# Attention outputs through HBM: new layouts, fewer stores, more loads, and the row maxima stored from ScalarE's queue

## What is computed

```python
content = einsum('bhqd,bhkd->bhqk', q, k)
relative = einsum('bhqd,qkd->bhqk', q, rpk)
w = softmax((content + relative) / sqrt(hd), axis=-1)
out = einsum('bhqk,bhkd->bhqd', w, v) + einsum('bhqk,qkd->bhqd', w, rpv)
x = x + layernorm(out @ Wo.T + bo)
x = x + layernorm(shared(layernorm(x)) + expert[top1](layernorm(x)))
```

## Time and profile before

| | |
|---|---|
| median of 3 runs | 1836.75 us (1835.77 to 1839.23) |
| profiled execution, its own time | 1832.55 us |
| its span, first to last instruction | 1830.8 us |
| granted TensorE clock, mean | 0.966 |
| busy: PE, DVE, ACT, POOL | 1635.2, 1253.0, 1108.6, 539.3 us |
| DMA packets, of these under 512 bytes | 490853, 332391 |

### The profile page before, as it was taken

One profiled execution on the slowest core, in us unless ns is written; L12 is line 12 of the kernel. 1 busy time (PEld: TensorE's weight loads), 2 busy tenths in 40 slices (PEclk: granted clock), 3 DMA queues, 4 the chain that ended last, 5 costly groups with the idle time before them and its releaser, 6 DMA issues. The chain is left out here.

```text
span 1830.8 us, 64404 instructions
## 1 busy us (share of the span) xinstructions
PE 1635.2 (89%) x26621; PEld 1211.2 (66%) x26621; DVE 1253.0 (68%) x3502; ACT 1108.6 (61%) x2059; POOL 539.3 (29%) x1114
## 2 busy tenths in 40 slices
PE   2889999999999999999999999999999897867772
PEld 1337767676777777767776777767677764567762
DVE  5996667787788878777878777868662344326655
ACT  2437767676767676767676766767556652256551
POOL 5423021314132313222331323131010126523445
PEclk9999999999999999999999999999999999979886
DMA  2468855755553554445344654463345533133340
GB/s 61 141 168 204 177 162 108 200 103 158 103 145 88 120 117 114 107 110 135 85 113 102 138 101 127 91 162 49 64 91 145 141 73 103 63 112 101 97 121 29
DMA packets 490853, 211.88 MB, mean 116 GB/s; under 512 B 332391, under 2 KB 464164, under 8 KB 490560
## 3 DMA queue, kind: packets, MB, share of 16 engines
q1 hardware_dynamic: 475968, 165.77, 40.5%
q0 software_dynamic: 14592, 42.00, 6.5%
HBM read 105.73 MB, written 102.85 MB: 114 GB/s over the span
## 5 line engine op out<-in xcount | busy, mean ns | idle before, releaser
L934 ACT ACTIVATE w<-sc,escale 128x512 f32<-128x512 f32 x1024 | 687.5, 687 | 424.5 <-PE sc L731 257.4
L1135 DVE TENSOR_REDUCE mx<-mix 128x1 f32<-128x512 f32 x960 | 647.0, 685 | 265.2 <-PE mix L711 239.8
L710 PE MATMUL mix<-WE 128*128 128x512 f16 x960 | 395.4, 412 | 23.3 <-DVE mx L1135 12.8
L724 PE MATMUL sc<-QC,KC 104*128 104x128 f16 x4096 | 401.9, 221 | 7.7 <-ACT w L934 4.5
L750 PE MATMUL pv<-w,VC 128*9 128x128 f32 x8192 | 385.8, 275 | 5.4 <-issue 5.3
L724 PEld LDWEIGHTS sc<-QC,KC 104*128 104x128 f16 x4096 | 271.3, 98 | 166.6 <-issue 81.1
L711 PE MATMUL mix<-Wn,WE 128*128 128x256 f16 (+1 forms) x960 | 290.0, 302 | 0.4 <-issue 0.4
L750 PEld LDWEIGHTS pv<-w,VC 128*9 128x9 f32 x8192 | 175.9, 90 | 150.8 <-issue 133.7
L757 PE MATMUL rel<-w,Rv 128*32 128x128 f32 x5120 | 264.7, 274 | 5.1 <-issue 5.1
L731 PE MATMUL sc<-QT,Wt 96*128 96x64 f16 x5120 | 262.0, 193 | 4.8 <-issue 4.6
L925 ACT ACTIVATE WE<-qp,hmask 128x256 f16<-128x256 f16 x512 | 249.1, 500 | 24.6 <-PE sc L711 21.2
(11 more groups left out here) (224 smaller groups left out, 1834.6 us busy)
## 6 DMA issues: line engine op xcount, KB each, us to landing
qm_d<-ks POOLq DMA_DIRECT2D x48, 512.0 KB, 4.2
QT<-qm_d SPq DMA_DIRECT2D x32, 768.0 KB
kt_d<-ks SPq DMA_DIRECT2D x48, 256.0 KB
KC<-kt_d SPq DMA_DIRECT2D x128, 96.0 KB
xs_d<-zrow SPq DMA_DIRECT2D x5, 2056.0 KB, 12.3
vs_d<-vst SPq DMA_DIRECT2D x16, 576.0 KB
VC<-vs_d SPq DMA_DIRECT2D x32, 288.0 KB
orl_d<-rel_s SPq DMA_DIRECT2D x512, 8.0 KB
```

The costliest lines, as they stand in the source:

```text
L710: nc.tensor.matmul(nat[:], lq, kn[b2][:, KEYS_AT[t]:KEYS_AT[t] + S], start=True, stop=False, skip_group_check=True)
L724: mm = nc.tensor.matmul(bank[:, P * g:P * g + P], KC[j][:, b2, g, 0 if near else 1, :], qc[:, g, :, 32 * q8:32 * q8 + 32], start=(g == 0), ...
L934: nc.scalar.activation(w[tile % 2][:, slot % 4, slot // 4 % 2].rearrange("p h q -> p (h q)"), sc[slot % 2][:], ACT.Exp, scale=escale[:, 0: ...
L1135: nc.vector.tensor_reduce(mx[:, k:k + 1], nat[:], AX.X, ALU.max).then_inc(s["mx_done"], 1)
```

## The change

Plain outputs and sums go to HBM with the head's dimension first (opv_d), four stores of 9 partitions a query tile instead of eight. The relative outputs go as rel_s stands, whole partitions, in one store of 128 partitions instead of sixteen of 8. A half is loaded with 12 transfers instead of 8: four for oB that pick the wanted partitions and queries (64-byte runs), two for oA, four for oS, two for xr. oA has rows ordered by dimension and head instead of head and dimension, so the rows of Wo are put in the same order once, by an ACT copy in the set-up for which PE waits. ACT writes pv_s in pieces of 128 elements; DVE reads rel in order and writes rel_s at a stride of 64 bytes. The sum of oA and oB is two instructions. The two stores of a group of row maxima leave SP's list for ACT's, behind the exponential of the same slot (slots 1 to 113 of the turns; the first pair's groups stay on SP).

```diff
-    opv_d = dram("opv_d", [B * H, HD + 1, S], F32)
-    orl_d = dram("orl_d", [B * H * HD, S], F32)
+    opv_d = dram("opv_d", [NP, NT, HD + 1, H, 2, P], F32)
+    orl_d = dram("orl_d", [NP, NT, P, H, NU, 2, NB], F32)
-    pv_s = sb("pv_s", [P, 2, 4, P])
-    rel_s = sb("rel_s", [P, NU, 2 * H, NB])
+    pv_s = sb("pv_s", [P, 4, 2, P])
+    rel_s = sb("rel_s", [P, H, NU, 2, NB])
+    wo_rows = w_flat[0][:, S * 4 - P:S * 4]
...
         def store_o(n, t):
 
             sp.wait_ge(s["pv_ev"], 2 * (4 * n + t) + 2)
-            rows = opv_d[bass.ds(2 * n * H, 2 * H)].rearrange("(b g hh) d q -> b g d hh q", b=2, g=4)
-            for b2 in range(2):
-                for g in range(4):
-                    sp.dma_start(rows[b2, g, :, :, P * t:P * t + P], pv_s[32 * g:32 * g + HD + 1, b2]).then_inc(s["o_st"], 16)
+            for g in range(4):
+                sp.dma_start(opv_d[n, t, :, 4 * g:4 * g + 4].rearrange("d h b q -> d (h b q)"),
+                             pv_s[32 * g:32 * g + HD + 1].rearrange("d h b q -> d (h b q)")).then_inc(s["o_st"], 16)
             sp.wait_ge(s["rel_ev"], 2 * (4 * n + t) + 2)
-            dst = orl_d[bass.ds(2 * n * P, 2 * P)].rearrange("(bh d) q -> d bh q", d=HD)
-            for q32 in range(NS):
-                for u in range(NU):
-                    row = 32 * q32 + HD * (NU - 1 - u)
-                    q0 = P * t + 32 * u + NB * q32
-                    sp.dma_start(dst[:, :, q0:q0 + NB], rel_s[row:row + HD, u, :, :]).then_inc(s["o_st"], 16)
+            sp.dma_start(orl_d[n, t].rearrange("p h u b k -> p (h u b k)"), rel_s[:].rearrange("p h u b k -> p (h u b k)")).then_inc(s["o_st"], 16)
...
             q = slice(S // 2 * half, S // 2 * (half + 1))
+            near = orl_d[n, 2 * half:2 * half + 2].rearrange("t (q v d) h u b k -> u v (d h) (t q) (b k)", v=NU, d=HD)
+            for u in range(NU):
+                sp.dma_start(oB[:, P * u:P * u + P].rearrange("p (n m) -> p n m", m=2 * NB), near[u, NU - 1 - u]).then_inc(s["o_ld"], 16)
             for b2 in range(2):
                 cols = slice(S // 2 * b2, S // 2 * (b2 + 1))
-                rows = opv_d[bass.ds((2 * n + b2) * H, H)]
-                sp.dma_start(oA[:, cols], rows[:, 0:HD, q]).then_inc(s["o_ld"], 16)
-                sp.dma_start(oB[:, cols], orl_d[bass.ds((2 * n + b2) * P, P), q]).then_inc(s["o_ld"], 16)
-                sp.dma_start(oS[:, cols], rows[:, HD:HD + 1, q].broadcast_to([H, HD, S // 2])).then_inc(s["o_ld"], 16)
+                plain = opv_d[n, 2 * half:2 * half + 2, :, :, b2]
+                sp.dma_start(oA[:, cols].rearrange("p (t q) -> p t q", t=2), plain[:, 0:HD].rearrange("t d h q -> (d h) t q")).then_inc(s["o_ld"], 16)
+                for t in range(2):
+                    sums = plain[t, HD]
+                    sp.dma_start(oS[:, cols][:, P * t:P * t + P],
+                                 bass.AP(sums.tensor, sums.offset, [[0, HD], *sums.ap])).then_inc(s["o_ld"], 16)
...
+        act.wait_ge(s["w_ld2"], 16 * MORE_LOADS)
+        nc.scalar.copy(wo_rows.rearrange("p (d h) -> p d h", d=HD), wraw[3].rearrange("p (h d) -> p d h", d=HD)).then_inc(s["wo_rdy"], 1)
...
-            nc.scalar.copy(pv_s[:, b2].rearrange("p h q -> p (h q)"), pv[b2][:]).then_inc(s["pv_ev"], 1)
+            nc.scalar.copy(pv_s[:, :, b2, :], pv[b2][:].rearrange("p (h q) -> p h q", q=P)).then_inc(s["pv_ev"], 1)
...
+        def store_max(n, b2, t):
+
+            group = NT * (2 * n + b2) + t
+            act.wait_ge(s["ms_done"], group + 1)
+            at_least(act, "ms_st", 32 * group)
+            dst = qt_d[bass.ds((2 * n + b2) * H, H)].rearrange("h r (t e b) -> r t e h b", t=NT, e=NE8)
+            for part in range(2):
+                act.dma_start(dst[ROWS_TERM + part, t], ms[:, part, 16 * t:16 * t + 16]).then_inc(s["ms_st"], 16)
+
         def turn(i, prev, nxt, nxt2):
             for slot in range(SLOTS):
                 exponentials(i, slot)
+                if slot == 1 and prev:
+                    store_max(i, 1, NT - 1)
+                if nxt and slot % 16 == 1 and slot > 1:
+                    store_max(i + 1, (slot // 16 - 1) // NT, (slot // 16 - 1) % NT)
...
-            nc.vector.tensor_copy(rel_s[:, :, :, 4 * half:4 * half + 4],
-                                  rel[half][:].rearrange("p (k c u) -> p u c k", k=4, u=NU)).then_inc(s["rel_ev"], 1)
+            nc.vector.tensor_copy(rel_s[:, :, :, :, 4 * half:4 * half + 4].rearrange("p h u b k -> p k b (h u)"),
+                                  rel[half][:].rearrange("p (k b n) -> p k b n", k=4, b=2)).then_inc(s["rel_ev"], 1)
...
-                dve.wait_ge(s["o_ld"], 128 * (c + 1))
-                plain = oA[:].rearrange("p (a n u) -> p a n u", n=P // NU, u=NU)
-                nc.vector.tensor_tensor(plain, plain, oB[:].rearrange("p (a u n) -> p a n u", n=P // NU, u=NU), ALU.add).then_inc(s["o_step"], 1)
+                dve.wait_ge(s["o_ld"], O_LOADS * (c + 1))
+                plain = oA[:].rearrange("p (b n k u) -> p b n k u", b=2, k=NB, u=NU)
+                near = oB[:].rearrange("p (u n b k) -> p b n k u", u=NU, b=2, k=NB)
+                for b2 in range(2):
+                    ins = nc.vector.tensor_tensor(plain[:, b2], plain[:, b2], near[:, b2], ALU.add)
+                ins.then_inc(s["o_step"], 1)
...
-O_STORES = 16 * (8 + 16)
+O_STORES = 16 * 5
+O_LOADS = 16 * (2 * 4 + NU)
```

More of the change, by code:

```diff
@@ L251, in attention_phase @@
     rel = [pb(f"rel{r}", [P, S]) for r in range(2)]
-    names = ("w_ld w_ld2 tab pool_set dve_set act_set pe_set sp_set wt_ld rv_ld zeroed kc_zeroed "
+    names = ("w_ld w_ld2 wo_rdy tab pool_set dve_set act_set pe_set sp_set wt_ld rv_ld zeroed kc_zeroed "
              "x_ld0 x_ld1 xn_step xn_done xT_ps xnT_rdy q_ps q_ev k_ps k_read k_ev v_ps v_ev qsplit ksplit "
@@ L558, in turn @@
                 if slot == 1:
-                    if prev:
-                        store_max(i, 1, NT - 1)
                     load_q(i, 1)
@@ L581, in turn @@
                         load_qn(i + 1, 1, slot // 64)
-                    if slot % 16 == 1 and slot > 1:
-                        store_max(i + 1, (slot // 16 - 1) // NT, (slot // 16 - 1) % NT)
                     if slot == 100:
@@ L683, in _ @@
         pe.wait_ge(s["w_ld2"], 16 * MORE_LOADS)
+        pe.wait_ge(s["wo_rdy"], 1)
         pe.wait_ge(s["dve_set"], SCALED)
-        for n in range(4):
+        for n in range(3):
             mm = transpose(sc[0][:, P * n:P * n + P], wraw[n])
+        mm = transpose(sc[0][:, 3 * P:4 * P], wo_rows)
         for n in range(4):
```

## The result

The changed kernel took 1851.35 us (median of 4 runs, 1849.29 to 1855.63), the kernel before 1836.26 beside it: ratio 1.0082, 95% interval 1.0060 to 1.0104, 15 us. The profiled execution took 1849.29 us, its span is 1847.6, against 1830.8.

A forecast was written before the change was run, and what follows sets the result against it. PE's own work, about 97% dense, was taken to bound the attention turns, not SP's queue. ACT's issues +2.5, DVE's copy +1 and the tail -1.5 sum to +2 on the 1836.75 us median: 1839 us, range 1827 to 1858.

The forecast's parts named there:

- no change: Whole kernel: time stays within 0.2% (3.7 us) of the kernel before; chance 0.38.
- full-queue rival: Row maxima's issues on ACT: ACT pays SP's full-queue price, +16 us (1852) up to +63 (1900); chance 0.15.
- the forecast's own case: Whole kernel: the summed forecast of 1839 us, own range 1834 to 1842; chance 0.40 together with all effects hidden.
- part 6: Small DMA packets of output stores and oB loads: PE starves in bursts, but the one inspected followed key stores; 0.
- signs that were to show a failure: Attention turns: PE's exponential waits grow over 1 us a turn, or its busy share moves over 2 us without them.
- Part 1: SP's queue: fewer output stores, more loads, 24.6 us of SP time saved a turn, valued at 0 inside turns.
- Part 2: Row maxima's 112 issues on ACT's queue delay exponentials: +2.5 us, lower bound 0, upper 9 a turn, 63 in all.
- standing ACT: Row maxima's issues on ACT: ACT stands still for two median issues without overlap, +5.5 us, 1841.5 to 1843; chance 0.17.
- Part 3: DVE's rel_s copy with strided writes: up to 0.64 us more each, 5.1 us a turn on DVE, mostly hidden; +1 us.
- Part 4: Tail after the last turn: SP reaches the remaining unit loads 5 us earlier, only part credited; -1.5 us.
- Part 5: Set-up: ACT's reordering copy of Wo's rows, at most 0.27 us, is covered by PE's wait for DVE; 0.
- the rival that I had built on it: PE's bursts of waiting: fewer small output packets shrink them, -6 to -8 us (1831), 1826 with the tail; chance 0.24.

The follow-up runs named there:

- e3: Changed kernel with the relative outputs stored in 16 parts of 8 partitions again, only the wanted values; ratio 1.0185 to the kernel before.
- e1: Changed kernel with the row maxima's stores put back on SP's queue; ratio 1.0054 to the kernel before.
- e2: Kernel before with only the row maxima's stores moved to ACT's queue; ratio 1.0028 to the kernel before.
- f1: Changed kernel with 8 of the 257 elements of each row scattered in the attention turns; one run, 1735.11 us.
- f3: Changed kernel with each scatter in the turns replaced by a plain transfer of the same 128 rows from POOL's queue; one run, 1732.35 us.

## Why the prediction held, and which of its steps didn't

The forecast was 1839 in 1827 to 1858, with "no change" as the likeliest case (0.38, against 0.36 for slower); 1851.35 lies in the range only by the width that rivals gave it, above all the full-queue rival, which didn't happen. That is luck: the forecast's own case reached to 1842. The likeliest case was wrong on the first chip, mainly in one step, part 6. The signs that were to show a failure would have missed it: over the whole run PE's waits for exponentials were 4.5 us before and 4.0 after, and from 652 to 829 PE was busy 0.6 us longer.

- **What bounds the kernel**: right. PE's own work sets the turns. By the measured issues SP's queue got back 4 x 7.5 - 2 x 2.3 = 25 us a turn, and no slot became shorter: other slots 839.7 and 840.0 us.
- **Part 1**: right in size (1.8 us of stores a tile, "about 2"), and right that it is worth 0 in a turn. I had missed that the whole rows are four times the bytes; in e3 the stretches are as long without them.
- **Part 2, +2.5 us**: the size is off; at the issues it is 0. Slots 16 to 24 take 11.5 us in each kernel, and the issue stands beside the engine's work, not in front of it. The rivals of a standing ACT (+5.5) and of a full queue (16 to 63 us) are out as well: an issue took 587 ns in the median and 1244 at most, where SP's reached 4852. The upper bound was also added up wrongly: six slots at 1.2 us and two at 1.7 are 10.6 us a turn and 74 in all, not 9 and 63; the range didn't hang on it. The first of the two issues started at 684.59, ahead of exponential 17 at 685.28 whose place in the list is before it: the sequencer had run ahead. The Trainium skill's run-ahead ("Perfetto Trace Analysis", section "Sequencer Loop") agrees with these rows. Of the 112 issues 88 overlapped SP's issuing, and their median is 587 ns, the same as that of the 24 which stood alone; six of the 88 took over 0.7 us, one of the 24 did. The Trainium skill's wait for a lock on the descriptor generator ("Perfetto Trace Analysis", section "DMA Instruction — HWDGE (DVE, Sync)") can show in those six at most.
- **Part 3, +1 us**: DVE's copy became 0.36 us longer (1042 against 681 ns), within the bound of 0.64, which is 2.9 us a turn on DVE. The slots outside the stretches hide it, and on chip E, where the copies are as long, the first stretch hides it too: 0. The Trainium skill's rule on cachelines ("SBUF — State Buffer", section "Specifications (TRN2)"), at least two hits on a line of 16 bytes, agrees for the write too: with each value in a line of its own the copy took 361 ns more, against the 636 ns that I took from the oB row.
- **Part 4, -1.5 us**: 0. SP came to the unit loads 4.1 us earlier after the last exponential (17.5 us behind it, 21.6 before), but oA plus oB started 26.5 and 26.6 us behind it, and behind the turns all took 343.3 us and 342.4. The finish chain there waits for unit work, as the step half said: the loads were issued by 1521.64, and DVE came to the sum behind a step of the units (L1375) for which it had waited 5.75 us.

```profile
1529.58 1.28 DVE L1375 TENSOR_TENSOR w<-w,pv 128x512 f32<-128x512 f32 x2 [5.75 <-ACT w L1015]
1530.79 1.11 DVE L1173 TENSOR_TENSOR oA<-oA,oB 128x256 f32<-128x256 f32 x2
```

- **Part 5, 0**: right. PE waited for DVE until 23.58, and ACT's copy of Wo ran at 16.29.
- **Part 6, 0**: this is the step that failed. "At that place SP had just stored keys, not outputs, so I leave it at 0" took the place of a stall in the program as proof that the change doesn't reach it. 15.5 of the 16.8 us came there, and as the opposite of the rival that I had built on it: the stalls became longer, not fewer. On chip E, where no stalls are, 0 was right.

What is shown: on chips A and C the changed kernel is slower, by ratios over repeated runs with intervals clear of 1, and in their profiles 15.5 of 16.8 and 16.3 of 17.3 us lie in the two stretches. The new layouts bring a loss without ACT's part (e1), ACT's part a smaller one without the layouts (e2), though no slot at ACT's issues from 16 to 24 is longer. The bytes of the whole rows and the key stores aren't needed for long stretches. On chip E, without stalls, the change gains 0.2%.

What stays open is how the change lengthens a stall. Hardly any of the changed transfers of outputs starts in a stretch: in turn 3 of the changed kernel the stores start in slots 10, 11, 43, 44, 72 to 74 and 105 to 107, the loads in slots 15 to 18 and 76 to 80. What else was changed and lies there are ACT's issues (slots 33 and 97), which by e1 aren't needed, the copies of ACT and DVE (slots 37 to 40) and the sum in two halves (slots 33, 34 and 94); none of these was tried alone. I compared where in the first stretch the scatters begin (slot 33 to 35 in the changed kernel, 33 to 37 before), and the stalls don't follow it: e3 begins in slots 33 to 36 and stalls as long. Whether the 12 loads, the stores or a copy do it wasn't tried apart. Nor is it settled that the scatters cause a stall, since f1 and f3 ran where there was none. A stretch of one and the same profile stands between 0 and 4.3 us over the shortest (kernel before, chip A), so part of the gap between single profiles can be chance. Over all of chips A, B and C, though, the five profiles with new layouts are all above the four without.

## What to carry to other kernels

Count a stall that is in the trace already as a resource of its own: an edit that leaves its transfers where they are can still make it longer, and a price of 0 for it needs a bound above. Issues from another engine's queue can be nearly free where that engine has work in flight and slack; look at the starts of the work behind, not at the length of the issue. Before a difference under 1% is explained, time both kernels on more than one chip, and profile both on each.

## What was not expected of the hardware

The kernel before took 1836 to 1848 us on three chips and 1736 and 1738 on two. The profiles have granted clocks of 0.966 on A, 0.958 on C (both of the kernel before) and 0.981 on E (the changed kernel). For the changed kernel on chip A and chip E the difference is 114 us in the span: 69 behind the turns, 36.5 in the stretches, 7.8 in the last turn, and 0.0 in the other slots (840.0 both). Behind the turns the clock stood at its lower level for 98.4 us on chip A and 56.0 on chip E; by estimate that explains at most half of the 42 us between them, 21 of the 69. In the experts' part the same matmul group shows it, chip A and chip E:

```profile
L1751 PE MATMUL gu<-sT,we 128*128 128x128 f32 x640 | 98.0, 302 | 44.0 <-ACT sT L1792 43.8
```

```profile
L1751 PE MATMUL gu<-sT,we 128*128 128x128 f32 x640 | 88.6, 282 | 3.8 <-ACT sT L1792 2.0
```

PE waited 44.0 us there on the one chip and 3.8 on the other. DMA packets were no slower: those of SP's queue from 300 to 1350 us took 28.9 ns in the mean on chip A and 29.0 on chip E, those of POOL's queue (scatters and query stores) 145 and 146. Behind the turns the means are 32.5 and 32.7 ns, 86.4 and 86.8. What delays PE and its semaphores on three of five chips stays open.
